# Decoder layer kernel: the cell's epsilon moved from VectorE into a ScalarE step, and four program orders changed

## The reference

```python
x = _layernorm(x + retention_and_conv(x))              # block 1
x = _layernorm(x + mlstm(q=x, k=ctx, v=ctx))           # block 2, 8 heads of 64
x = _layernorm(x + moe(x))                             # block 3, 32 experts, top 2
...
# in block 2, per head:
normalizer = jnp.maximum(jnp.abs(C.sum(axis=-1, keepdims=True)), jnp.exp(-max_log_D))
h = jnp.einsum('hst,htd->hsd', C / (normalizer + EPS), vh)
...
# in block 3, after the experts' rows are computed:
out = jnp.zeros((T, C), xf.dtype).at[idx.reshape(-1)].add((w[..., None] * ye).reshape(-1, C))
```

## Time and profile before

| what | value |
|---|---|
| median of 3 runs | 1650.98 us (1650.79 to 1651.0) |
| profiled execution, its own time | 1650.46 us |
| profiled execution, span | 1648.7 us |
| TensorE matmul busy | 1473.0 us, 89% of the span |
| VectorE busy | 935.2 us, 57% |
| ScalarE busy | 498.6 us, 30% |
| GpSimd busy | 307.7 us, 19% |

### The profile page before, as it was taken

How to read it: one execution, slowest core, us unless ns; L and a number is a source line. 1 busy time by engine, 2 the same in 40 slices (tenths; PEclk the granted TensorE clock), 3 DMA queues, 4 the chain that set the end, 5 groups by cost and what they waited for, 6 DMA issues and landing times.

```text
span 1648.7 us, 29396 instructions
## 1 busy us (share of the span) xinstructions
PE 1473.0 (89%) x10924; PEld 1127.8 (68%) x10924; DVE 935.2 (57%) x2764; ACT 498.6 (30%) x1187; POOL 307.7 (19%) x397
## 2 busy tenths in 40 slices
PE   5689999999989721799999999999999999999996
PEld 3355556556556411678888788887887878878884
DVE  8567999999988889332423334234333242332455
ACT  4556676675755552001001010010010100101023
POOL 4012121121112200112121121121211212112125
PEclk9689999999999755799999999999999999999998
DMA  6203313132130261177676776767767777677696
GB/s 179 71 21 102 78 65 102 54 95 71 66 89 2 102 290 54 29 293 260 244 289 217 292 271 226 295 229 282 274 220 293 244 266 282 216 295 255 250 353 221
DMA packets 92289, 310.71 MB, mean 188 GB/s; under 512 B 42807, under 2 KB 46781, under 8 KB 82877
## 3 DMA queue, kind: packets, MB, share of 16 engines
q1 hardware_dynamic: 79260, 287.87, 47.5%
q0 software_dynamic: 12960, 21.96, 5.9%
HBM read 273.18 MB, written 36.63 MB: 188 GB/s over the span
## 4 chain that ended last, share of the span: by engine, by line
PE 69%; DVE 17%; ACT 5%; issue 5%; DMA 3%; POOL 1%; SPq 1%; POOLq 0%; DVEq 0%; ACTq 0%
PE bank L1053 36%; PE banks L1067 14%; PE bank L678 5%; PE banks L1070 4%; DVE arena L1531 3%; PE banks L780 2%; DVE arena L1993 2%; DVE arena L1521 1%; PE bank L680 1%; ACT arena L1262 1%; DMA acc_rows<-arena,keep 1%; DMA arena<-acc_rows 1%; PE banks L791 1%; ACT arena L1193 1%; DVE arena L1571 1%
## 5 line engine op out<-in xcount | busy, mean ns | idle before, releaser
L1465 ACT ACTIVATE arena<-bank 128x160 f32<-128x160 f32 x288 | 87.1, 303 | 871.6 <-PE bank L1053 861.7
L1053 PE MATMUL bank<-keep,arena 128*128 128x160 f32 x2304 | 320.0, 299 | 1.5 <-DVE arena L2247 1.5
L1053 PE MATMUL bank<-arena 128*128 128x160 f32 x2304 | 320.0, 301 | 0.9 <-issue 0.9
L1053 PEld LDWEIGHTS bank<-arena 128*128 128x128 f32 x2304 | 316.2, 191 | 4.2 <-issue 4.2
L1053 PEld LDWEIGHTS bank<-keep,arena 128*128 128x128 f32 x2304 | 315.4, 189 | 5.4 <-issue 3.2
L2247 DVE TENSOR_TENSOR arena<-arena,bank 128x160 f32<-128x160 f32 x256 | 82.1, 321 | 405.2 <-ACT arena L1465 353.1
L1067 PE MATMUL banks<-arena 128*128 128x512 f32 x558 | 244.6, 592 | 0.0
L2437 POOL DMA_INDIRECT acc_rows<-arena,keep x62 | 99.1, 1598 | 624.9 <-DVE arena L2142 612.7
L1067 PEld LDWEIGHTS banks<-arena 128*128 128x128 f32 x558 | 104.3, 190 | 118.7 <-issue 118.6
L2140 DVE TENSOR_SCALAR arena<-banks,keep 128x512 f32<-128x512 f32 x31 | 23.2, 750 | 184.5 <-PE banks L1070 184.5
L678 PE MATMUL bank<-arena 128*128 128x512 f32 x224 | 104.6, 609 | 6.5 <-DVE arena L1531 6.5
(11 more groups left out here) (318 smaller groups left out, 1822.8 us busy)
## 6 DMA issues: line engine op xcount, KB each, us to landing
arena<-in_wup SPq DMA_DIRECT2D x32, 4096.0 KB, 12.6
arena<-in_wdn SPq DMA_DIRECT2D x32, 2048.0 KB
arena<-in_aup SPq DMA_DIRECT2D x32, 512.0 KB, 11.7
arena<-in_xT SPq DMA_DIRECT2D x32, 256.0 KB, 3.0
arena<-in_kT SPq DMA_DIRECT2D x8, 1024.0 KB, 6.1
arena<-in_v SPq DMA_DIRECT2D x32, 256.0 KB, 6.7
x_rows<-arena SPq DMA_DIRECT2D x8, 1024.0 KB, 4.5
acc_rows<-arena SPq DMA_DIRECT2D x8, 1024.0 KB, 6.8
```

The source lines that it names most:

```text
L1053: m = pe.matmul(u[:, g * CAP:(g + 1) * CAP], w, xeT[e.slot][:, c, :], start=(c == 0), stop=(c == C - 1))
L1465: act.activation(sg[k], Ub[k][:, 0:CAP], ACT.Silu).then_inc(up_a(f"silu{j}"), 1)
```

## The change

Four things are changed.

1. ScalarE adds the epsilon to the floor `en` once per batch (a new instruction with a step `floor`, in place). VectorE's `head_out` then needs four instructions for each pair: max(eps - s, floor + eps), then max(s + eps, that), reciprocal, multiply.
2. VectorE's `scale_queries(n-1, 1)` stands ahead of `norm1_stats(n, 3)`, no longer behind `head_out(n-1, 0)`.
3. VectorE's `router_signs(n-2)` stands behind `weigh(n-1, 3)`, no longer ahead of `scale_queries(n-1, 2)`.
4. In the tail, GpSimd makes the shifts of batches 6 and 7 ahead of the second `redone_gather`, and `last_root(1)` ahead of `redone_scatter`; VectorE normalises batch 7 first and scales the last expert's part rows (`last_part`) ahead of `redone_out`; SyncE stores batch 7 ahead of batch 6.

```diff
@@ ScalarE, gates_5
                 act.activation(wcol, cols[:, :, 64:64 + NH], ACT.Exp).then_inc(ga_a("w"), 1)
+                act.wait_ge(*ga_a.at("en", b))
+                act.activation(en[b.slot], en[b.slot], ACT.Copy, bias=CELL_EPS).then_inc(ga_a("floor"), 1)
@@ VectorE, head_out
-                    dve.wait_ge(*ga_a.at("en", b))
+                    dve.wait_ge(*ga_a.at("floor", b))
...
-                dve.scalar_tensor_tensor(den, pv[:, :, :, DH], -1.0, floor, ALU.mult, ALU.max).then_inc(ev_v(f"neg{j}"), 1)
+                dve.scalar_tensor_tensor(den, pv[:, :, :, DH], CELL_EPS, floor, ALU.subtract, ALU.max, reverse0=True)\
+                    .then_inc(ev_v(f"neg{j}"), 1)
                 dve.wait_ge(*ev_v.at(f"neg{j}", b))
-                dve.tensor_tensor(den, pv[:, :, :, DH], den, ALU.max).then_inc(ev_v(f"den{j}"), 1)
+                dve.scalar_tensor_tensor(den, pv[:, :, :, DH], CELL_EPS, den, ALU.add, ALU.max).then_inc(ev_v(f"den{j}"), 1)
                 dve.wait_ge(*ev_v.at(f"den{j}", b))
-                dve.tensor_scalar(den, den, CELL_EPS, None, ALU.add).then_inc(ev_v(f"eps{j}"), 1)
-                dve.wait_ge(*ev_v.at(f"eps{j}", b))
                 dve.reciprocal(den, den).then_inc(ev_v(f"rec{j}"), 1)
@@ VectorE, step
                 if s:
                     weigh(n - 1, 1)
+                if s:
+                    scale_queries(n - 1, 1)
                 if a and s:
                     norm1_stats(n, 3)
                     norm1(n)
                 if s:
                     head_out(n - 1, 0)
-                    scale_queries(n - 1, 1)
...
-                if r:
-                    router_signs(n - 2)
...
                 if s:
                     scale_queries(n - 1, 2)
                     weigh(n - 1, 3)
+                if r:
+                    router_signs(n - 2)
@@ SyncE, the stores
-            for b in range(NB):
+            for b in (*range(NB - 2), NB - 1, NB - 2):
@@ VectorE, the last expert
                 if last:
+                    last_normalised()
                     redone_statistics(0)
-                    last_normalised()
+                    last_part(e)
                     redone_out(0)
@@ GpSimd, the tail
             redone_gather(0)
-            redone_gather(1)
             for n in range(6, NB):
                 shifts(n)
+            redone_gather(1)
             redone_root(0)
+            last_root(1)
             redone_scatter()
-            last_root(1)
             last_scatter()
```

More of the change, by code:

```diff
@@ L357, in decoder_kernel @@
         ga_t = steps("gate_tensor", ["gates_k", "parts", "gates", "cols"])
-        ga_a = steps("gate_scalar", ["parts", "ig", "abs", "relu", "exp", "log", "hi", "m0", "mid", "gcol", "en", "w", "F", "Fhi", "Fm", "Fmid"])
+        ga_a = steps("gate_scalar", ["parts", "ig", "abs", "relu", "exp", "log", "hi", "m0", "mid", "gcol", "en", "w", "floor", "F", "Fhi", "Fm", "Fmid"])
         ga_v = steps("gate_vector", ["cum", "g", "max", "neg", "r1", "lo", "Fr", "Flo"])
@@ L370, in decoder_kernel @@
         st_v = steps("state_vector", ["vw", "m1", "S1", "m2", "S2"])
-        ev_v = steps("ev_vector", [x for j in range(NP) for x in (f"neg{j}", f"den{j}", f"eps{j}", f"rec{j}", f"out{j}")])
+        ev_v = steps("ev_vector", [x for j in range(NP) for x in (f"neg{j}", f"den{j}", f"rec{j}", f"out{j}")])
         l2_v = steps("ln2_vector", ["bn2", "aggr2", "scaled", "sum", "bn3", "aggr3"])
@@ L2191, in lanes, with last_part, last_rows @@
                                   ALU.mult, ALU.add).then_inc(le_v("idx"), 1)
-            def last_rows(e):
+            def last_part(e):
+                w = w_l[:, 2 * NE - 1:2 * NE]
+                dve.wait_ge(*lr_t.at("y1", b0))
+                dve.tensor_scalar(yy[e.slot][:, D:], Yb[1][:, 0:P], w, None, ALU.mult).then_inc(lr_v("y1"), 1)
+            def last_rows():
                 w = w_l[:, 2 * NE - 2:2 * NE]
-                dve.wait_ge(*lr_t.at("y1", b0))
-                dve.tensor_scalar(yy[e.slot][:, D:], Yb[1][:, 0:P], w[:, 1:2], None, ALU.mult).then_inc(lr_v("y1"), 1)
                 dve.wait_ge(ld_r[1], 32)
@@ L2268, in _ @@
             run_experts(dve, expert)
-            last_rows(Batch(0, NE - 1))
+            last_rows()
         @block.gpsimd
```

## The result

| | before | changed |
|---|---|---|
| median | 1650.9 us (4 runs, 1650.79 to 1651.0) | 1668.22 us (4 runs, 1666.47 to 1670.57) |
| ratio, 95% interval | | 1.0107 (1.0095 to 1.0119) |
| profiled execution, its own time | 1650.46 us | 1667.3 us |
| profiled execution, span | 1648.7 us | 1665.5 us |
| VectorE busy | 935.2 us | 930.0 us |

The kernel became 1.1% slower, 17.3 us, where 4.6 were forecast. The direction was right and the size was not: the time lies 8.7 us above the range. Two things stand out in the table. VectorE has less work, as it should, yet TensorE, whose program did not change, is busy 10.7 us longer. And the four runs lie 4.1 us apart, those of before 0.2; in the larger sets of the experiments, 8 to 31 runs each, the kernel before spreads over 1.2 to 5.8 us itself.

A forecast was written before the change was run, and what follows sets the result against it. In step 5 neither VectorE nor TensorE was taken to bound the kernel alone; a chain through several engines mattered. Terms 0.15 + 1.8 + 2.05 + 0.56 + 0 = +4.6 us gave 1655.6 us, range 1652.0 to 1659.5.

The forecast's parts named there:

- The stall: Ahead of the fourth tile's statistics: scaling waits for TensorE's L652, VectorE stands 1.42 us longer; `values` of pair 1 waits 2 us.
- A middle step is 0.41 us longer: Steps 2 to 6: gate chain 0.85 us later, pairs 2 and 3 give back 0.44; five steps make +2.05.
- the case without a stall: Rival, chance 0.07: `f1` is there when VectorE comes; a middle step gains 1.24 us, total about 1643.9.
- VectorE's and TensorE's ledgers: Middle steps: TensorE's `values` of pair 1 1.64 us later; VectorE 1.18 later at L1706, 0.96 after pair 1.
- the meeting of the two at `weigh` of pair 3: VectorE comes at 367.06, but late scores let `weigh` start only at 367.32, against 366.55 before: +0.77 us.
- the clock falls too: Rival, chance 0.08: TensorE's idle of about 2 us ahead of `values` halves its rate; 1 us more each step, about 1662.
- Step 1: TensorE and ScalarE's chain sets the gate chain's start, so 1.64 us arrives whole; with ScalarE's epsilon instruction +1.8.
- Step 7: TensorE nearly without a gap before `broadcast_max(n, 0)`: 1.44 us passes on, pairs take off 0.22 and 0.66: +0.56.
- The tail: Stores after the last expert: last store issued 1.8 us earlier, but DMA engines full; taken as 0, bounds -1.8 and +0.8.
- only one dip: DMA engines full from the store of batch 5 on, with a single dip, to share 0.74, at 1628.5.
- The sum: Whole kernel: 0.15 + 1.8 + 2.05 + 0.56 + 0 = +4.6 us, giving 1655.6.

The follow-up runs named there:

- both fillers: Changed kernel plus ten repeated TensorE matmuls ahead of `values` of pair 1 and eight at the start of each step 1 to 7: 1659.15 us, ratio 1.0048.
- ten matmuls in the idle: Changed kernel plus ten repeated TensorE matmuls between scores of pair 2 and `values` of pair 1, filling the idle: 1656.28 us, ratio 1.0033.
- experiment 5: Kernel before with the epsilon's edits alone, 1648.04 us; with the sign sums' move alone, 1647.12; with both, 1646.18; before 1651.11.
- experiment 6: Kernel before with the tail's edits alone (SyncE, GpSimd, last expert on VectorE): 1652.08 us against 1651.11, ratio 1.0006.
- the last kernel: Kernel before with epsilon and sign sums moved, plus eight repeated TensorE matmuls at each step's start from step 3 on: 1643.35 us, ratio 0.9949.

## Why the prediction was wrong in size

- **The stall** (part 2): right. The scaling waits 2.36 us for L652, the statistics follow at once, `values` of pair 1 waits 2.00.
- **"A middle step is 0.41 us longer"**: right where the clock held, 0.49 and 0.45 in the changed kernel, 0.47 in the one with both fillers. The gain of the case without a stall, 1.24, was measured as 1.3. VectorE's and TensorE's ledgers, and the meeting of the two at `weigh` of pair 3, were worked out rightly. Step 2, which the prediction counted as a middle step, isn't one: with ten matmuls in the idle it is 63.08 against 63.00, +0.08.
- **The step that failed** is the rival *the clock falls too*, given 0.08 and "each step would cost 1 us more: about 1662". It is what happened, in five of seven steps, and its price was wrong too. "If half rate held for two or three such groups a step" set the price; in step 5 the half rate held for 6.8 us, through most of `values`, the broadcasts and all sixteen transposes of the queries, and put the broadcast of pair 2 back by 2.1 us. That wait is VectorE's next, so 2.1 of it arrived whole in step 5; in step 1, where TensorE's chain is the pace anyway, the period grew by 3.4 more than forecast. Over the seven steps the falls cost 12.2 us, by the periods with ten matmuls in the idle.
- **Why it was weighed so low.** The clock of before was 1.00 in the whole of step 5, and I took this as evidence for the changed kernel. But a fall from 321.7 to 325.1 us lies just ahead of that window, and the window held no idle of 2 us at `values`: the wait there was 0.35 us. Elsewhere the trace of before had such idles and falls behind them, and the prediction looked at none of these places but step 1 (2.39 us against 2.00). TensorE of before, at the start and at the end of step 3:

```profile
194.29 5.40 PE L678 MATMUL bank<-arena 128*128 128x512 f32 x8 [1.88 <-DVE arena L1531]
...
256.42 0.24 PE L732 MATMUL bank<-arena 72*128 72x2 bf16 x4 [1.42 <-DVE arena L1685]
256.59 2.67 PE L742 MATMUL bank<-arena 128*64 128x65 f32 x48
```

  The first eight L678 take 5.40 us there and 3.71 in step 6, behind the same idle. That fall lies in the one middle period of before that is longer, 66.34 us against 65.26 to 65.29: it had a price, 1.07 us, that could have been read. Of the three idles of 1.88 or 1.89 us ahead of L678 in that trace (steps 3, 6 and 7) it is the only one with a fall. The fall behind L732, and the like one at 321.7, lie in periods of 65.26 and 65.28 and cost nothing: VectorE's taps set the pace at that place, and TensorE only idles 0.41 us ahead of the next L678 instead of 1.89. The prediction also read the Trainium skill ("TensorE: Matmul & The Clock Gate", section "HAM oscillation") too widely. That section has a kernel whose engine falls back to half rate at every one of its waits, but these are DMA waits of some 3 to 5 us; for 2 us it decides nothing. Here 2.00 us were enough in five steps of seven, and not in the other two.
- **Step 1** ("+1.8"): +5.20. The stall's share is as forecast (TensorE's L780 waits 2.00 us there too); the rest is the clock, since with ten matmuls in the idle the period is 60.03, +1.72.
- **Step 7** ("+0.56"): +1.75 with a fall; with both fillers the period is 65.69, shorter than before. The term was too high: the signs' move helps there by itself, as experiment 5 showed.
- **The tail** ("I take 0; bounds -1.8 and +0.8"): 1.65 us longer in this profile, 0.95 on average over five profiles each, unresolved in the times. All of it lies ahead of the output scatters. The upper bound of 0.8 was too narrow: it counted bytes that move; a gap between the transfers is the likely term (experiment 6). The reading "only one dip" was wrong as well. Windows of before, behind the store of batch 5 (issued at 1624.23):

  ```profile
1624.50:1625.00 0.50, 0.50 (x3) 0.26 (x2) 0.00 (x0) 0.00 (x0) 0.42 (x2) 1.00 0.71 90
1625.00:1625.50 0.50, 0.50 (x3) 0.07 (x1) 0.37 (x1) 0.40 (x1) 0.34 (x3) 1.00 0.70 107
```

- **The sum** at a held clock was 1655.6; the kernel that holds it at the stall measured 1656.3. That they lie so close is partly luck: in its profile the tail adds 1.06 us, the way from the last gate chain to the experts 1.0 and one fall at a step's start 1.27, none of which was in the sum, while steps 2, 3 and 7 are 0.3, 1.0 and 1.3 us below their terms (step 3 because before has a fall there).

## What to carry to other kernels

When an edit makes TensorE wait, don't price the wait alone: look in the trace of before for idles of the same length, wherever they are, and see what the granted clock did behind them. Price a fall by all the work behind it that runs at half rate until the next cross-engine wait, here 1.9 to 3.5 us a step for a wait of 2.0. An engine that would idle can be kept at its clock by repeating a harmless matmul into a bank that is free, but only where it would truly idle: in the two steps where it did not, the repeats cost 2.8 us.

## What was unexpected in the hardware

The same idle had two outcomes. Ahead of `values` TensorE waited 2.00 us in all seven steps of one execution; its clock fell to 1.2 GHz at five of these waits and stayed at 2.4 at two. With the queries alone moved the waits there were 2.2 us, and it fell at four of seven. At the steps' starts 1.88 or 1.89 us of idle was followed by a fall in some steps only, and 1.24 us ahead of `values` by a fall in four steps of seven. Behind 0.89 us there was none in the seven steps of one profile. What decides between the two outcomes is open.

The falls don't explain how far the runs of a kernel lie apart. The changed kernel's four lie 4.1 us apart and those with both idles filled 0.9, but the last kernel, whose profile has no fall in steps 3 to 7 either, spreads over 5.7 us in five runs, and the kernel before over 1.2 to 5.8 us in sets of 8 to 31.
